# Filter matrices laid in SBUF during the first phase, in a one-core decoder kernel

## The reference, cut to what matters

```python
i_ = jnp.arange(chunk)                       # chunk = 32
inv = -(kb @ jnp.swapaxes(k, -1, -2)) * strict_lower
for i in range(1, chunk):
    inv = inv.at[..., i, :].add(jnp.einsum('...j,...jk->...k', inv[..., i, :], inv))
inv = inv + jnp.eye(chunk, dtype=q.dtype)
...
long[t, c]  = sum(fir_long[c, j]  * v[t - 63 + j, c] for j in range(64))
short[t, c] = sum(fir_short[c, j] * v[t -  4 + j, c] for j in range(5))
```

## Time and profile before

| what | us |
|---|---|
| median of 3 runs | 1322.98 (1320.78 to 1327.27) |
| the profiled execution, its own time | 1323.56 |
| its span, first to last instruction | 1321.8 |
| phase A, by the trace | 0 to 240.4 |
| phase B | 240.7 to 319.5 |
| phases CX and F | 319.7 to 1321.8 |

### The profile page before, as it was taken

One profiled execution on the slowest core, in us unless ns is written; L12 is line 12 of the kernel. 1 busy time (PEld: TensorE's weight loads), 2 busy tenths in 40 slices (PEclk: granted clock), 3 DMA queues, 4 the chain that ended last, 5 costly groups with the idle time before them and its releaser, 6 DMA issues. The chain is left out here.

```text
span 1321.8 us, 28637 instructions
## 1 busy us (share of the span) xinstructions
PE 1119.9 (85%) x9251; PEld 820.2 (62%) x9251; DVE 958.0 (72%) x2132; ACT 898.0 (68%) x1743; POOL 653.0 (49%) x2200
## 2 busy tenths in 40 slices
PE   5998988783678799999999999999999888885756
PEld 4776766683566566766776776676677655443225
DVE  5999998698355657777877877777787566633985
ACT  5999998221344558787878878877887665453867
POOL 4777775563225544465465466547546543111007
PEclk9999998555557869999999999999999988897989
DMA  2443433893412434343433434343442342203106
GB/s 80 159 176 144 177 136 144 185 234 107 137 57 85 110 80 127 95 124 109 133 110 106 146 105 138 106 129 105 111 144 82 96 127 57 65 33 140 44 1 223
DMA packets 141779, 154.17 MB, mean 117 GB/s; under 512 B 48040, under 2 KB 106560, under 8 KB 141632
## 3 DMA queue, kind: packets, MB, share of 16 engines
q1 hardware_dynamic: 141632, 152.35, 38.4%
HBM read 93.32 MB, written 58.72 MB: 115 GB/s over the span
## 5 line engine op out<-in xcount | busy, mean ns | idle before, releaser
L2120 DVE TENSOR_REDUCE x_maxima<-x_psA 128x2 f32<-128x512 f32 x248 | 170.3, 687 | 96.2 <-PE x_psA L1448 93.7
L1704 ACT ACTIVATE x_PT<-x_psB 128x512 f32<-128x512 f32 x240 | 143.0, 596 | 56.5 <-PE x_psB L1472 52.1
L1711 ACT ACTIVATE x_psA<-x_mask_q 128x512 f32<-128x512 bf16 x239 | 142.4, 596 | 51.8 <-DVE x_maxima L2120 48.7
L297 DVE SCALAR_TENSOR_TENSOR a_conv<-a_ps_proj,taps,a_conv 128x253 f32<-128x253 f32 (+2 forms) x288 | 115.0, 471 | 8.4 <-ACT a_conv L364 8.4
L1448 PE MATMUL x_psA<-x_Ks,x_Qs 96*128 96x256 bf16 x496 | 99.5, 283 | 15.2 <-ACT x_psA L1711 14.7
L1469 PE MATMUL x_psB<-x_mask_k,x_ident_bf 128*128 128x512 bf16 x240 | 94.3, 393 | 13.0 <-ACT x_PT L1704 10.8
L533 PE MATMUL a_ps_proj<-a_hT,wqkv 128*128 128x256 f32 x384 | 93.2, 392 | 7.1 <-DVE a_conv L297 4.2
L1472 PE MATMUL x_psB<-x_Qs,x_Ks 98*128 98x256 bf16 x480 | 94.1, 277 | 0.0
L533 PEld LDWEIGHTS a_ps_proj<-a_hT,wqkv 128*128 128x128 f32 x384 | 71.5, 194 | 19.4 <-issue 6.6
L1864 POOL TENSOR_SCALAR x_parts_q<-x_rest 128x512 bf16<-128x512 f32 x16 | 23.9, 1494 | 116.3 <-DVE x_rest L2096 116.3
L1486 PE MATMUL x_psO<-x_PT,x_V 128*32 128x256 f32 x1024 | 72.0, 401 | 1.0 <-ACT x_PT L1704 1.0
(11 more groups left out here) (390 smaller groups left out, 3352.8 us busy)
## 6 DMA issues: line engine op xcount, KB each, us to landing
scratch_keypack<-a_keypack SPq DMA_DIRECT2D x16, 768.0 KB, 3.3
c_keypack<-scratch_keypack SPq DMA_DIRECT2D x16, 768.0 KB, 4.7
x_Ks<-scratch_k_parts SPq DMA_DIRECT2D x192, 64.0 KB, 2.2
b_matrix<-in_long_padded SPq DMA_DIRECT2D x16, 512.0 KB, 7.4
scratch_k_parts<-x_parts_k SPq DMA_DIRECT2D x32, 192.0 KB, 2.4
scratch_q_parts<-x_parts_q SPq DMA_DIRECT2D x32, 192.0 KB, 2.3
x_Qs<-scratch_q_parts SPq DMA_DIRECT2D x32, 192.0 KB, 3.0
a_x_in<-in_x SPq DMA_DIRECT2D x16, 256.0 KB, 2.7
```

The costliest lines, as they stand in the source:

```text
L297: nc.vector.scalar_tensor_tensor(acc, ps_proj[PROJ_BANK[p]][:, c, 0:L - j], taps[:, p, c, TAPS - 1 - j:TAPS - j], acc, ALU.mult, ALU.add). ...
L1704: nc.scalar.activation(PT[:, k % (2 * GROUP)], bank_B(b, k)[0], ACT.Exp, scale=XD ** -0.5).then_inc(pexp_ready, 1)
L1711: nc.scalar.activation(psA[:].rearrange("p t q -> p (t q)"), mask_q[:, k % 2].rearrange("p s k -> p (s k)"), ACT.Copy).then_inc(mask_writt ...
L2120: nc.vector.tensor_reduce(maxima[:, t, 2 * pair:2 * pair + 2], bank_A(b, k)[0], AX.X, ALU.max).then_inc(maxed, 1)
```

## The change

- v stays in token order. `v_windows[:, 1]` is now the copy of v itself (ACT, `vtok`), and SP fills `v_windows[:, 0]`, which holds v shifted by 64 tokens, with two SBUF-to-SBUF DMAs per sequence (`win`). The reversal matrices, `flipA`, `flipB`, `fA`, `fB` and `a_v_tok` go.
- At the start of A one DMA writes 16 copies of each channel's padded taps (192 floats) to a DRAM scratch tensor. Per sequence, SP then issues one DMA (`taps`, stage 1) of 16 partitions, every eighth one, and 128 channels; 16 of them fill `matrix`, which holds all 256 channels' matrices with the reversal in them.
- Phase B loads no matrices. PE does one multiplication of 64 columns per channel; the two halves of the channels go to the two halves of the output partitions; eight groups of PSUM instead of four. All of SP's early loads stand at the start; `long_all` goes out in 8 stores in place of 2, in runs of 256 bytes instead of 512.
- To make room, `diag` is kept in `X32`, three quarters of `M` and `product` live there too, and `lower`, `squares` and `short_tok` in `shared`. Transposes in and out now wait for one another, and POOL's chain waits for all four instead of one.

The diff, cut to its core:

```diff
@@ A_ORDER
-(4, "norm"), (2, "turn_h"), (2, "hTc"), (5, "flipA"), (4, "ktok"), (5, "st_p"), (4, "st_k"),
-(3, "conv_q"), (5, "diag"), (4, "stap"), (5, "dk"), (5, "fA"), (3, "tanh"), ...
+(4, "norm"), (2, "turn_h"), (2, "hTc"), (4, "ktok"), (5, "st_p"), (4, "st_k"), (1, "taps"),
+(3, "conv_q"), (5, "diag"), (4, "stap"), (5, "dk"), (3, "tanh"), ...
-(4, "st_v"), (3, "tok0"), ... (4, "flipB"), ... (4, "fB"), (3, "sq1"),
+(4, "st_v"), (4, "win"), (3, "tok0"), ... (3, "sq1"),
@@ phase_a, sync
+                elif op == "taps":
+                    row, half = b // FC, b % FC
+                    sp.wait_ge(taps_copied, 16)
+                    taps_of = bass.AP(dram["taps_copies"].tensor, half * P * COPIES * FIR_COLS + P - 1 - row,
+                                      [[FIR_COLS - STEP, COPIES], [COPIES * FIR_COLS, P], [1, HB]])
+                    sp.dma_start(keep["matrix"][row:P:STEP, half * P:half * P + P], taps_of).then_inc(taps_placed, 16)
+                elif op == "win":
+                    sp.wait_ge(v_tok_ready, b + 1)
+                    sp.dma_start(keep["v_windows"][HB:P, 0, :, b], keep["v_windows"][0:HB, 1, :, b]).then_inc(window_set, 16)
+                    sp.dma_start(keep["v_windows"][0:HB, 0, 1, b], keep["v_windows"][HB:P, 1, 0, b]).then_inc(window_set, 16)
-            sp.dma_start(flip[:], dram["flip"]).then_inc(w_loaded, 16)
-            sp.dma_start(half_flip[:], dram["half_flip"]).then_inc(w_loaded, 16)
+            sp.dma_start(dram["taps_copies"], bass.AP(dram["long_padded"].tensor, 0, [[FIR_COLS, D], [0, COPIES], [1, FIR_COLS]])).then_inc(taps_copied, 16)
@@ phase_b
+        M_first = sb("M_first", [P, 1, CH, CH])
+        M_rest = keep["X32"][:, 0:(NQ - 1) * CH].rearrange("p (q i) j -> p q i j", q=NQ - 1)
+                for i in range(CG):
+                    for half in range(FC):
+                        c = half * P + group * CG + i
+                        last = nc.tensor.matmul(psum[n][half * HB:half * HB + HB, i], keep["matrix"][:, c],
+                                                keep["v_windows"][:, :, :, :, c].rearrange("p a t b -> p (a t b)"),
-            pool.wait_ge(M_turned, 1)
+            pool.wait_ge(M_turned, NQ)
+            for q in range(NQ):
+                if q > 0:
+                    dve.wait_ge(M_turned, q)
```

More of the change, by code:

```diff
@@ new lines, in _ @@
+            sp.dma_start(early["k_tok"][:, 0], dram["k_tok"][0]).then_inc(early["pack_loaded"], 16)
+            sp.dma_start(early["hT0"][:], dram["hT"][0]).then_inc(early["hT_loaded"], 16)
+            sp.dma_start(keep["shared"][:, 0, 0], dram["v_tok"][0]).then_inc(early["vs_loaded"], 16)
+            sp.dma_start(keep["shared"][:, 0, 1], dram["short_tok"][0]).then_inc(early["vs_loaded"], 16)
+            for stage in range(2):
+                sp.wait_ge(kept, (stage + 1) * (GROUPS // 2))
+                for half in range(FC):
+                    for part in range(2):
+                        at = slice(half * P + stage * HB, half * P + stage * HB + HB)
+                        sp.dma_start(dram["long_tok"][part * HB:part * HB + HB, :, :, at].rearrange("p t b c -> p (t b) c"),
+                                     keep["long"][half * HB:half * HB + HB, part, :, stage * HB:stage * HB + HB]).then_inc(long_stored, 16)
@@ L679, in _ @@
                 n = group % DEPTH
-                pe.wait_ge(loaded[n], 16 * (group // DEPTH + 1))
                 if group >= DEPTH:
                     pe.wait_ge(kept, group - DEPTH + 1)
-                for c in range(CG):
-                    for part in range(2):
-                        last = nc.tensor.matmul(psum[n][part * HB:part * HB + HB, c].rearrange("p t b -> p (t b)"),
-                                                matrix[n][:, c], keep["v_windows"][:, part, :, :, group * CG + c].rearrange("p t b -> p (t b)"),
+                for i in range(CG):
+                    for half in range(FC):
+                        c = half * P + group * CG + i
+                        last = nc.tensor.matmul(psum[n][half * HB:half * HB + HB, i], keep["matrix"][:, c],
+                                                keep["v_windows"][:, :, :, :, c].rearrange("p a t b -> p (a t b)"),
                                                 start=True, stop=True, skip_group_check=True)
@@ L695, in _ @@
                 act.wait_ge(filtered, group + 1)
-                out = keep["long"][:, :, :, group * CG:(group + 1) * CG].rearrange("p t b c -> p (t b) c")
-                nc.scalar.activation(out, psum[n][:].rearrange("p c t b -> p (t b) c"), ACT.Copy).then_inc(kept, 1)
+                out = keep["long"][:, :, :, group * CG:(group + 1) * CG].rearrange("p a n c -> p (a n) c")
+                nc.scalar.activation(out, psum[n][:].rearrange("p c n -> p n c"), ACT.Copy).then_inc(kept, 1)
                 if group == EARLY_AT + 2:
```

160 lines of the change are left out of this document (58 added, 102 removed).

## The result

The changed kernel takes 1341.3 us, median of 4 runs (1340.34 to 1345.67); the kernel before, run beside it, 1324.16 (1320.78 to 1327.27). The ratio is 1.0136, interval 1.0101 to 1.0171. The forecast was 1334, the sum behind it +11.0 us. The profiled execution of the changed kernel took 1342.18 us, its span is 1340.4, which is 18.6 longer than that of before.

What follows compares the result with a forecast made beforehand. POOL's chain of dependent small operations, 13.23 us a sequence, was taken to bound phase A, DVE phase B. The terms -1.5 + 11.1 + 1.4 = +11.0 on 1323.56 give 1334.6, predicted as 1334; range 1325.6 to 1344.

Steps and rivals of the forecast that it cites:

- The start, the copy: Start of phase A: copy landed at 22.4, x of sequence 2 waits behind it; 11.1 us lost.
- Reversals removed, steady part: Phase A's periods: 25 us of work leave ACT, PE loses its reversals; cost nothing, covered by POOL's chain of 13.23 us.
- the clock falls: Rival, chance 0.05: without reversals PE falls to 1.2 GHz in phase A and passes POOL's 13.23 us; +30, 1365 us.
- The 67% window: Phase A of the kernel before: PE's granted clock was 1.00 also while 67% busy, taken as evidence against a clock fall.
- The end of A: Phase A's end: last diagonal blocks move up 0.9 us, the last `v_windows` copy of 0.6 goes; 1.5 us gained.
- The other DMAs in phase A: Phase A: 16 `taps` and 32 window DMAs on SP's queue, which stays under 0.8; cost zero.
- Phase B: Transposes waiting +1.5, memsets +0.2, constants' wait -0.75, DVE's operations beside POOL +0.4; sum 1.4 us lost, bounds 0 to 4.
- slow copy: Rival, chance 0.17: at the start of phase A the copy lands at 29, at its upper end; 1341.5 us.
- CX and F: Phases the change does not touch: predicted difference 0; moving by more than 3 us would show the prediction wrong.

Runs made afterwards that it cites:

- e2: The changed kernel with the copy issued behind the first `hT` store and the `taps` loads in stage 4 instead of 1; 1328.36 us, ratio 1.0036.
- e4: The changed kernel with PE's reversal multiplications put back as dummies that nobody reads, no copies by ACT; 1334.63 us, ratio 1.01.
- e5: The changed kernel with the edits of e2, e3 and e4 together; 1318.83 us, ratio 1.0022 against the kernel before.
- e1: The kernel before with the reversals alone taken out, no new DMA; 1328.17 us, ratio 1.0038.
- e3: The changed kernel with PE starting phase B's filter only when all transposes in are done; 1343.95 us, ratio 1.0154.
- e11: e5 without PE's dummy reversals; 1324.6 us, ratio 1.0053 against the kernel before.
- e10: e1 with DVE's six short-filter steps made products of one SBUF input, the short filter's sums left out; 1319.83 us, one run.

## Why the prediction was right and wrong, step by step

- **The start, the copy: right.** Landed at 21.5 against 22.4, x 27.8 predicted, `stat` at 28.10, the first convolution at 29.19 against 29.1. e2 shows it (-12.2 on the first `ks`) to hang on SP's early wait for the copy. Mis-sized in its last step: "I take off 0.5 for small gaps behind it that close" should have been an addition of 2, as PE stood idle and began again at the low clock (6.67 us for 16 records, 4.10 for the 16 from 20.52 before). Of the 2.7 us missed here up to 1.5 can be that mark's scatter.
- **"Reversals removed, steady part: I cost them at nothing": the step that failed**, by +7.7 us. That ACT's 25 us are worth nothing was right (e4, e5). That the cover, "POOL's chain of 13.23 us, which contains none of it and waits for none of it", holds was not: POOL waits for none of it, but its operations' durations follow where DVE's fall. e1 shows 3.3 us of the loss with the reversals alone gone (197.6), the other 4.4 need the early copy too (e2), and e4 shows nearly all of it gone with the multiplications alone back (195.3). What the list of waits could not tell is that a POOL operation's own duration depends on DVE's beside it: it listed eight kinds of wait, none over 0.2 us (not seven, as the prediction counts), and no hold, because a hold is inside the busy time. The prediction read the waits and not the spread of durations of one form.
- **Rival "the clock falls", 0.05: its mechanism came, its price did not.** The clock fell to 0.83 to 0.97 in 20 us windows, but PE did not become the bound; +7.7 instead of +30. The 67% window, on which I had discounted this rival, did not carry over. The Trainium skill (TensorE: Matmul & The Clock Gate, Why this matters for your kernels) has the rule that gaps between bursts bring the low clock back. The fall agrees with its warning, but not through longer gaps: from 140 to 200 us PE's longest listed wait is 1.1 us in e1 and 1.3 in the kernel before, and the granted clock (last but two) is 0.89 in the first row, of e1, and 1.00 in the second, of before.

```profile
140.00:200.00 60.00, 54.98 (x328) 45.59 (x327) 53.95 (x140) 48.96 (x115) 44.05 (x157) 0.89 0.43 159
```

```profile
140.00:200.00 60.00, 53.84 (x353) 42.02 (x352) 56.13 (x145) 54.58 (x126) 42.38 (x152) 1.00 0.40 146
```

- **The end of A: right.** 8.4 to 6.9, -1.5.
- **"The other DMAs in phase A: cost zero": right.** The DMA share rose to between 0.66 and 0.82 from 80 us on, the stores of `hT` land after 5.4 us, and the periods of e2 are those of e1. With the early copy this is not tested.
- **Phase B: the sum right for what it counted, its terms less so.** With PE out of the way B is 80.1 to 80.2 in e3, e5 and e11, +1.4 to +1.5. But the eight transposes in and out gave 0.7 of that (7.74 + 7.72 in e3 against 7.65 + 7.10), not 1.5. The wait of 0.75 went, as expected, and DVE's operations of the 30 steps add up to 73.2 us in e3 where they were 71.5, +1.7 in place of +0.4; why is open. Missed was that PE's filter stretches the transposes in, +2.3. Before, PE began that filter at 245.02, 4.3 us behind DVE, and of the four transposes the median took 1.89 and only the longest 2.24.
- **Rival "slow copy": wrong.** The copy landed at 21.5, near the forecast and far from 29. Its 13.1 us to landing are also less than the estimated 17.6 us of data by the figure of the Trainium skill (HBM Reference, Specifications). That figure is a core's share with both cores of a pair at work, and this program has one core; for such a copy the measurement decides against it.
- **"CX and F" moved by 5.2**, over the 3 us set as a mark. In the spans of the table they lie between 994.6 and 1002.3 without order by edit, and a kernel's own runs scatter by as much (1320.78 to 1327.27 for before). By the traces the difference is there after 193 us of CX, in which the granted clock rises from 0.50 to about 0.8; whether the moment at which PE enters CX sets it was not tried and stays open.
- The total was 7 us above the forecast, in the range: the terms missed (+2.7, +7.7, +2.4) add to 12.8, and 5.2 came back by the scatter of CX and F. That the time lies in the range is luck in part: without these 5.2 it would be about 1346.5, above the range's end at 1344.

One more difference fits a fall of the clock: of PE's waits for POOL's `ks`, 60 to 200 us, the longest is 3.7 us in place of 1.3. So a held POOL operation makes PE idle for longer, which may bring the low clock, which shifts DVE, which holds POOL again. But this circle isn't what starts the fall: from 140 to 200 us e1 has no held record and no wait of PE over 1.1 us, and its clock is 0.89 all the same. What is shown is the two ends: PE's 2.1 us of reversals a sequence gone, and POOL's operations recorded longer. It is shown too that dummies of the same length bring clock and period back. That the clock is the link between them, and not the changed times in PE's queue, is argued and stays open.

## What to carry to other kernels

Work taken from an engine off the critical path isn't free of effect: here PE's reversals, needed by nobody's chain, kept the clock at 1.00 and the order in which DVE and POOL met, and without them the kernel was 0.4% slower (e1). Before calling an engine's chain self-contained, look at the shortest, median and longest duration of one form of its operations: a spread (0.22, 0.31, 0.53 us) is a wait that no list of waits shows. And a wait on an in-order DMA queue costs the load queued behind it: issue a large first copy where nothing urgent follows, as e2 did: 12.9 us back, of which the first `ks` has 12.2 in the profile.

## What the runs showed of the hardware

- A small POOL operation that meets certain DVE operations is recorded as long: 0.22 us alone, 0.31 to 0.34 beside the two-input steps of the short filter, 0.69 beside one addition of 0.68, and 2.34 to 2.54 when held over a whole group of six steps; 1.57 and 1.58 over a group of six with one input (e10). Beside the convolutions (L297, which read PSUM), the statistics and the reductions of the kernel before none is longer than alone. The Trainium skill (SBUF — State Buffer, SBUF: two separate sides) tells of an exclusive lock on the pair of ports that DVE and POOL share, taken by a DVE operation with two SBUF inputs or in a mode that uses both ports, for the length of one instruction. The meetings with two-input operations agree. The holds across six instructions on end (e1, 128.62; e10, 154.41) are longer than that sentence has it, and whether the one-input steps ran in such a mode no run here shows.
- DVE's transposes of 128x1024 took 1.90 to 1.92 us each with PE idle and 2.44 to 2.78 with PE's filter running (e3 against after). The Trainium skill (SBUF — State Buffer, SBUF: two separate sides) states that PE, ACT and DVE's own ports never wait on anyone; for these transposes the runs show otherwise. Whether it is the reading of SBUF or the instructions' supply that is shared was not tried.
- A copy of 3072 KB from DRAM to DRAM, in 768-byte pieces, landed 13.1 us after its issue.
- Adding some 2.1 us of useless PE work per 13.2 us, with the granted clock at 1.00 in place of 0.83 to 0.97, took 6.7 us off the fifteen periods (202.0 to 195.3) and as much off the medians (1341.3 to 1334.63, four runs each).
